# Three blocks of a selective scan: where GpSimd's additions and TensorE's convolution stand in the order of the state stage

## The chip, the cores and the metric

One core of a Trainium2 chip. The metric is the device time of one execution of the whole program in microseconds, median of the runs.

## What is computed

An image batch x of 16 x 28 x 28 x 32 passes through four layers, each added to x and each fed by a group norm of it: window attention, a gated convolution with a selective state space, a triangle product, and a gated recurrence. The change is in the second layer alone. Cut to what matters, for a sequence of L = 784 positions, D = 32 channels, N = 8 states:

```python
x1 = silu(conv3x3_depthwise(grouped_1x1(x, w1)))
u, z = in_proj(x1)
u = silu(causal_conv1d(u, 3 taps) + conv1d_b)
dt, Bm, Cm = split(u @ x_proj_w.T)
delta = softplus(dt @ dt_proj_w.T + dt_proj_b)
# for each position, in order:
h = exp(delta * A) * h + (delta * u) * Bm        # D x N
y = sum_n(h * Cm)
# behind the scan:
y = (y + u * D_param) * silu(z)
x1 = layernorm(out_proj(y)) * gamma + beta
out = grouped_1x1(x1 * silu(grouped_1x1(x, w2)), wout)
```

## The kernel before

Partitions are 4 groups of 32 channels, each group with images of its own, so the 16 images are four blocks of T = 784 columns. In the state stage, about 135 to 285 us of the span, the blocks c = 0..3 follow each other, and each has eight slots n = 0..7, one for each state. Slot (c, n) is:

- TensorE, `spread(c, n, h)`, L1339: row n of B spread over the channels, a matmul for each half h of the columns. It reads BCf, the rows of B and C of a block, in three bfloat16 pieces, and waits for `g_low`, the last step of `split(c)`. Half 0 also waits for the first scan half of the slot before, half 1 for its second (both blocks share one place in PSUM).
- VectorE, `times_b` (L1965) and `scan` (L1977), for each half: DU times the spread row in place, then the scan with the decay dA as factor. The first half also needs the decay from ScalarE (`decays`, L826) and that product n of four slots ago has been taken.
- DMA: `c_rows` on the SP queue (L428) copies row n of C out of BCf to all 32 channels of each group, 392 KB, into one of four buffers Cs. It waits for the product of four slots ago. Between these issues stand the twelve copies SX<-XP (L418) that each later block's 3x3 convolution reads.
- GpSimd, `times_c(c, n)`, L534: hC = Hs x Cs. It needs the row (`s_cs`), the scan (`v_s`) and the total of three slots ago (`y_s`). In this document it is product (c,n).
- TensorE, `total(c, n)`, L1343: hC added up over n in PSUM. When total(c,7) is done, VectorE's `outputs(c)` reads the sum (L1994, then L1997).

Everything that the next block needs is made beside these slots: on TensorE conv (L1278, 24 matmuls a half, from 12 in the program), inner (L1290), gate, delta, x_b (L1263, L1303), each put by hand between spreads and totals; on ScalarE their activations, each group behind a load of its table. Softplus of block k is made of max(v, 0), log(u) with u = 1 + exp(-|v|), and the rounding rest of u: `remainder(k)` on VectorE (L1942) gives `rest`; GpSimd adds the logarithm (`plus_log`, L539) and then subtracts the rest (`delta`, L544, which releases `v_dl`). `v_dl` is what the decays of block k and VectorE's `delta_u(k)` (L2006: DU = DL x US) wait for. GpSimd's `split(k)` (L518, L520) makes the three pieces of B. `scaled` (L551) and VectorE's `norm` (L1988), which waits for it, belong to the layer norm of the block two back, `residual` to its output.

Each engine runs its own list in the written order, and each waits by semaphores alone, so where a step stands in a list decides what is held up behind it. GpSimd's list between product (i,4) and product (i,7) was:

```python
# i = 0: 4, 5, plus_log(1), delta(1), split(1), 6, 7
# i = 1, 2: 4, split(i+1), plus_log(i+1), delta(i+1), 5, 6, scaled(i-1), 7
```

VectorE has delta_u(1) behind slot (0,7) in block 0, and delta_u(i+1) between slots (i,6) and (i,7) in blocks 1 and 2.

Of the kernel before, what the change touches and what calls it, by code (L numbers as in the profile page):

```python
# [8 lines left out]
ALU = mybir.AluOpType  # L9
# [31 lines left out]
def build(nc, a, out):  # L41
    ctx = ExitStack()
    with ctx:
# [423 lines left out]
        def _(eng):  # L467
# [46 lines left out]
            def split(k):  # L514

                eng.wait_ge(c_["xB"], k + 1)
                two, one = BCf[0:2 * C, k % 2, :], BCf[0:C, k % 2, :]
                eng.tensor_tensor(two, two, upper(two), ALU.subtract).then_inc(g_mid, 1)  # L518
                eng.wait_ge(g_mid, k + 1)
                eng.tensor_tensor(one, one, upper(one), ALU.subtract).then_inc(g_low, 1)  # L520
# [15 lines left out]
            def plus_log(k):  # L536
                eng.wait_ge(a_m, k + 1)
                eng.wait_ge(a_l, k + 1)
                eng.tensor_tensor(DL[:, k % 2, :], DL[:, k % 2, :], sp[:, SP_L, :], ALU.add).then_inc(g_ml, 1)  # L539

            def delta(k):
                eng.wait_ge(v_cc, k + 1)
                eng.wait_ge(g_ml, k + 1)
                eng.tensor_tensor(DL[:, k % 2, :], DL[:, k % 2, :], rest, ALU.subtract).then_inc(v_dl, 1)  # L544
# [41 lines left out]
            def pool_ssm(i):  # L586
                if i < J - 1:
                    times_c(i, 0, 1, 2, 3, 4)
                    if i == 0:
                        times_c(0, 5)  # L590
                        plus_log(1)
                        delta(1)
                        split(1)
                    else:
                        split(i + 1)
                        plus_log(i + 1)
                        delta(i + 1)
                        times_c(i, 5)
                    times_c(i, 6)
# [43 lines left out]
        def _(eng):  # L643
# [237 lines left out]
            def act_ssm(i):  # L881
                if i == 0:
# [14 lines left out]
                    decays(1, 0, 1)  # L897
# [4 lines left out]
                    decays(1, 2, 3)  # L902
# [181 lines left out]
        def _(eng):  # L1084
# [293 lines left out]
            def pe_ssm(i):  # L1378

                if i == 0:  # L1380
# [29 lines left out]
                    total(0, 4)  # L1410
                    spread(1, 0, 0)
                    conv(2, 1)
                    spread(1, 0, 1)
                    total(0, 5)
                elif i == 1:
                    spread(1, 1, 0)
                    inner(2, 0)
                    spread(1, 1, 1)
                    inner(2, 1)
                    spread(1, 2, 0)  # L1420
                    total(0, 6)
                    spread(1, 2, 1)
                    total(0, 7)
                    gate(1)
                    spread(1, 3, 0)
                    delta(2, 0)
                    delta(2, 1)
                    spread(1, 3, 1)
# [839 lines left out]
```

## Time and profile before

| | us |
|---|---|
| Median of 3 runs (all: 428.93, 429.76, 434.81) | 429.76 |
| The profiled execution | 428.19 |
| Its span, first to last instruction | 426.2 |
| TensorE busy in the span | 370.1 |
| VectorE busy | 315.3 |
| ScalarE busy | 286.0 |
| GpSimd busy | 163.2 |

The profile has the span, and 2.0 us of the execution's time lie around it. Engines in its rows: PE is TensorE, PEld its weight loads, DVE VectorE, ACT ScalarE, POOL GpSimd, SP the queue that issues DMAs. L534 is line 534 of the program.

### The profile page before, as it was taken

To read this page: it belongs to the slowest core of one execution; us is meant where nothing else is said; L and a number is where in the kernel's file an instruction comes from. 1 tells how busy PE (TensorE), PEld (TensorE's weight loads), DVE (VectorE), ACT (ScalarE), POOL (GpSimd) and SP (SyncE) were. 2 spreads that over 40 slices of the span, in tenths; PEclk is the share of its full clock that TensorE was granted. 3 is DMA by queue.
4 is the path that set the end of the run, shared out by engine and by line. 5 is a ranking of instruction groups with operands and counts; after the bars stand their busy time and mean duration, and the time that the engine had idled before them with its cause. 6 is when DMAs were issued, how large, how long until landed. Compare 5 with 4: busy or idle time off the path is not lost.

```text
span 426.2 us, 11110 instructions
## 1 busy us (share of the span) xinstructions
PE 370.1 (87%) x4065; PEld 252.5 (59%) x4065; DVE 315.3 (74%) x637; ACT 286.0 (67%) x600; POOL 163.2 (38%) x138
## 2 busy tenths in 40 slices
PE   5889999999998797698898776898978989999996
PEld 5667777777764342254354342443954569888885
DVE  2889886788746899589799899895658957555554
ACT  3599899999858684559859773359974354444443
POOL 7314313323103256755974988961622400000000
PEclk9999999999999999699999996999999989999999
DMA  7120000004133354263222222200020001111111
GB/s 160 9 21 7 2 0 1 0 0 100 32 70 89 118 137 123 109 163 114 102 101 104 102 98 102 75 0 0 11 67 2 2 1 23 16 22 22 22 22 27
DMA packets 28671, 23.17 MB, mean 54 GB/s; under 512 B 21105, under 2 KB 22897, under 8 KB 28641
## 3 DMA queue, kind: packets, MB, share of 16 engines
q1 hardware_dynamic: 28244, 22.73, 19.5%
q8 instruction: 18, 0.29, 0.3%
q10 hardware_dynamic: 396, 0.05, 0.1%
q14 instruction: 13, 0.10, 0.1%
HBM read 2.00 MB, written 1.61 MB: 8 GB/s over the span
## 4 chain that ended last, share of the span: by engine, by line
PE 35%; DVE 28%; issue 17%; ACT 9%; POOL 7%; DMA 3%; DVEq 1%; SPq 1%; ACTq 0%; POOLq 0%
PE pair L1670 7%; DVE pair L1965 5%; DVE Ts L1856 3%; PE pair L1658 3%; PE pair L1126 3%; PE pair L1177 3%; DVE stats L1744 3%; PE pair L1166 2%; DVE Hs L1977 2%; PE pair L1290 2%; PE pair L1185 2%; PE pair L1278 2%; DMA vec<-in_L_conv_b_qkv 2%; PE pair L1148 2%; POOL hC L534 2%
## 5 line engine op out<-in xcount | busy, mean ns | idle before, releaser
L534 POOL TENSOR_TENSOR hC<-Hs,Cs 128x784 f32<-128x784 f32 x31 | 63.5, 2051 | 44.2 <-DVE Hs L1977 27.3
L502 POOL TENSOR_TENSOR Km<-Ks,mask 128x784 f32<-128x784 f32 x16 | 24.1, 1506 | 68.7 <-ACT Ks L709 68.7
L1343 PE MATMUL pair<-hC,ident 128*128 128x392 f32 x128 | 49.2, 509 | 0.0
L1850 DVE TENSOR_REDUCE mx<-pair 128x8 f32<-128x392 f32 x64 | 32.9, 555 | 16.3 <-PE pair L1126 16.2
L1965 DVE TENSOR_TENSOR pair<-DU,pair 128x392 f32<-128x392 f32 x64 | 35.5, 555 | 8.9 <-PE pair L1339 8.8
L1339 PE MATMUL pair<-BCf,sel 96*128 96x392 bf16 x64 | 21.9, 348 | 22.5 <-DVE Hs L1977 17.9
L1166 PE MATMUL pair<-ident,Pr 128*128 128x128 f32 x256 | 37.5, 279 | 2.4 <-issue 1.2
L1670 PE MATMUL pair<-hst,BD 128*128 128x112 f32 x224 | 37.6, 299 | 2.2 <-DVE Rt L2237 0.4
L1166 PEld LDWEIGHTS pair<-ident,Pr 128*128 128x128 f32 x256 | 28.2, 141 | 13.2 <-issue 12.2
L1977 DVE TENSOR_TENSOR_SCAN Hs<-dA,Hs,pair 128x392 f32<-128x392 f32 x32 | 32.9, 1030 | 3.6
L1670 PEld LDWEIGHTS pair<-hst,BD 128*128 128x128 f32 x224 | 30.0, 195 | 9.3 <-DVE hst L2231 5.5
L826 ACT ACTIVATE dA<-DL,Aneg 128x784 f32<-128x784 f32 x32 | 29.1, 941 | 7.9 <-POOL DL L544 6.3
L1977 DVE TENSOR_TENSOR_SCAN Hs<-dA,pair 128x392 f32<-128x392 f32 x32 | 31.1, 970 | 4.2
L1339 PEld LDWEIGHTS pair<-BCf,sel 96*128 96x128 bf16 x64 | 6.2, 98 | 46.9 <-issue 39.2
L696 ACT ACTIVATE Pr<-Ts 128x392 f32<-128x392 f32 x64 | 31.5, 547 | 3.2 <-DVE Ts L1856 2.5
L1658 PE MATMUL pair<-XN,BD 128*128 (+1 forms) x224 | 31.8, 286 | 1.8 <-ACT XN L1047 1.8
L1343 PEld LDWEIGHTS pair<-hC,ident 128*128 128x128 f32 x128 | 24.7, 197 | 14.4 <-issue 4.2
L1856 DVE TENSOR_TENSOR Ts<-pair,mx 128x392 f32<-128x392 f32 x64 | 32.8, 553 | 0.0
L687 ACT ACTIVATE PT<-pair 128x392 f32<-128x392 f32 x64 | 29.6, 496 | 4.1 <-PE pair L1166 3.0
L1658 PEld LDWEIGHTS pair<-XN,BD 128*128 128x128 f32 x224 | 28.0, 196 | 2.3 <-ACT XN L1047 2.3
L1067 ACT ACTIVATE gates<-pair 128x112 f32<-128x112 f32 x28 | 7.4, 263 | 29.0 <-PE pair L1670 29.0
L2218 DVE SCALAR_TENSOR_TENSOR prods<-gates 128x112 f32<-128x112 f32 x28 | 7.7, 275 | 24.1 <-ACT gates L1067 24.1
(254 smaller groups left out, 842.1 us busy)
## 6 DMA issues: line engine op xcount, KB each, us to landing
Cs<-BCf SPq DMA_DIRECT2D x32, 392.0 KB
SX<-XP SPq DMA_DIRECT2D x48, 112.2 KB
XT<-in_x SPq DMA_DIRECT2D x4, 392.0 KB, 6.8
out<-Os SPq DMA_DIRECT2D x28, 56.0 KB, 1.7
AD<-Aa SPq DMA_DIRECT2D x4, 196.0 KB
NB<-in_L_conv_x_proj_w SPq DMA_DIRECT2D x4, 3.0 KB
DW<-in_L_conv_dw SPq DMA_DIRECT2D x4, 1.1 KB
W<-in_L_conv_w_qkv ACTq DMA_DIRECT2D x1, 48.0 KB
```

What stands on the lines that cost most here:

```text
L534: eng.tensor_tensor(hC[:, i % NHC, :], Hs[:, i % NHS, :], Cs[i % NCS][:, :], ALU.mult).then_inc(v_c, 1)
L687: eng.activation(PT[:, g].rearrange("p a b (o q) -> p (a b o) q", o=2), banks[5 + (par + 1 + g) % 2][:, :].rearrange("p (m k) -> p m k", k ...
L696: eng.activation(Pr[:, par, g, :, 0:WT], Ts[:, g, :, :], ACT.Exp).then_inc(exp_r, 1)
L826: eng.activation(dA[:, n % NA, :], DL[:, c % 2, :], ACT.Exp, scale=Aneg[:, n:n + 1]).then_inc(a_da, 1)
L1166: ins = eng.transpose(bk[:, P * k:P * k + P], pg, ident[:, :])
L1343: return eng.matmul(STATES[:, h, :], ident[:, :], src[:, columns(h)], start=first, stop=last)
L1658: eng.matmul(zb[k].rearrange("p (b n) -> p b n", b=J), BD[:, U_X + k, :], xt, start=False, stop=False, skip_group_check=True)
L1670: eng.matmul(zb[k], BD[:, U_M + k, :], hst[:, 1 - par, :], start=False, stop=True, skip_group_check=True).then_inc(done, 1)
L1850: eng.tensor_reduce(mx[:, g, :], banks[g][:, 0:392].rearrange("p (m k) -> p m k", k=WT), AX.X, ALU.max).then_inc(max_r, 1)
L1856: eng.tensor_tensor(Ts[:, g, :, :], banks[g][:, 0:392].rearrange("p (m k) -> p m k", k=WT), bcast(mx[:, g, :], 2, WT), ALU.subtract).then_ ...
L1965: eng.tensor_tensor(SPREAD[:, columns(h)], DU[:, c % 2, columns(h)], SPREAD[:, columns(h)], ALU.mult).then_inc(v_b, 1)
L1977: eng.tensor_tensor_scan(Hs[:, i % NHS, columns(h)], dA[:, n % NA, columns(h)], SPREAD[:, columns(h)], h0, ALU.mult, ALU.add).then_inc(v_s, 1)
```

## The change

GpSimd's order: at every boundary the two softplus additions come right behind product (i,4), then the split, then products 5, 6 and 7. In block 0 product (0,5) stood ahead of them; in blocks 1 and 2 the split did. The two additions change places: the rest is subtracted first, which needs `remainder`, and the logarithm is added last, which needs ScalarE's logarithm; the last still releases `v_dl`. The sum is the same up to rounding.

ScalarE: the decay (1,2) stands ahead of the silu group instead of behind it.

TensorE: between the spreads of slots (1,0), (1,1) and (1,2) the convolution of block 2 no longer stands as a whole half. conv(2,1) is put in three single taps (8 of the 24 matmuls each), inner(2,0) and inner(2,1) in two taps and one tap, and totals (0,5) to (0,7), gate(1) and delta(2) move by one place.

```diff
--- before.py
+++ after.py
@@ -533,15 +533,15 @@
                         eng.wait_ge(y_s, i - NHC + 1)
                     eng.tensor_tensor(hC[:, i % NHC, :], Hs[:, i % NHS, :], Cs[i % NCS][:, :], ALU.mult).then_inc(v_c, 1)
 
-            def plus_log(k):
+            def minus_rest(k):
                 eng.wait_ge(a_m, k + 1)
+                eng.wait_ge(v_cc, k + 1)
+                eng.tensor_tensor(DL[:, k % 2, :], DL[:, k % 2, :], rest, ALU.subtract).then_inc(g_ml, 1)
+
+            def delta(k):
                 eng.wait_ge(a_l, k + 1)
-                eng.tensor_tensor(DL[:, k % 2, :], DL[:, k % 2, :], sp[:, SP_L, :], ALU.add).then_inc(g_ml, 1)
-
-            def delta(k):
-                eng.wait_ge(v_cc, k + 1)
                 eng.wait_ge(g_ml, k + 1)
-                eng.tensor_tensor(DL[:, k % 2, :], DL[:, k % 2, :], rest, ALU.subtract).then_inc(v_dl, 1)
+                eng.tensor_tensor(DL[:, k % 2, :], DL[:, k % 2, :], sp[:, SP_L, :], ALU.add).then_inc(v_dl, 1)
 
             def scaled(m):
 
@@ -586,17 +586,10 @@
             def pool_ssm(i):
                 if i < J - 1:
                     times_c(i, 0, 1, 2, 3, 4)
-                    if i == 0:
-                        times_c(0, 5)
-                        plus_log(1)
-                        delta(1)
-                        split(1)
-                    else:
-                        split(i + 1)
-                        plus_log(i + 1)
-                        delta(i + 1)
-                        times_c(i, 5)
-                    times_c(i, 6)
+                    minus_rest(i + 1)
+                    delta(i + 1)
+                    split(i + 1)
+                    times_c(i, 5, 6)
                     if i:
                         scaled(i - 1)
                     times_c(i, 7)
@@ -894,12 +887,12 @@
                     copy_bc(1)
                     exponents()
                     decays(0, 7)
-                    decays(1, 0, 1)
+                    decays(1, 0, 1, 2)
                     silu_x2(1)
                     silu_conv(2, 0)
                     silu_conv(2, 1)
                     exponents()
-                    decays(1, 2, 3)
+                    decays(1, 3)
                 elif i < J - 1:
                     if i == 2:
                         silu_x2(2)
@@ -1408,24 +1401,28 @@
                     conv(2, 0)
                     spread(0, 7, 1)
                     total(0, 4)
+                    conv(2, 1, (0,))
                     spread(1, 0, 0)
-                    conv(2, 1)
+                    conv(2, 1, (1,))
                     spread(1, 0, 1)
+                    conv(2, 1, (2,))
                     total(0, 5)
                 elif i == 1:
                     spread(1, 1, 0)
-                    inner(2, 0)
+                    inner(2, 0, (0, 1))
                     spread(1, 1, 1)
-                    inner(2, 1)
+                    inner(2, 0, (2,))
+                    total(0, 6)
                     spread(1, 2, 0)
-                    total(0, 6)
+                    inner(2, 1, (0, 1))
                     spread(1, 2, 1)
+                    inner(2, 1, (2,))
                     total(0, 7)
+                    spread(1, 3, 0)
                     gate(1)
-                    spread(1, 3, 0)
                     delta(2, 0)
+                    spread(1, 3, 1)
                     delta(2, 1)
-                    spread(1, 3, 1)
                     total(1, 0)
                     spread(1, 4, 0)
                     x_b(2)
```

## Rows read from the trace of the kernel before

**Rows 1.** The page's part 4, the chain that ended last: shares by engine.

```profile
PE 35%; DVE 28%; issue 17%; ACT 9%; POOL 7%; DMA 3%; DVEq 1%; SPq 1%; ACTq 0%; POOLq 0%
```

**Rows 2.** Stretches: us, busy of PE, PEld, DVE, ACT, POOL, PEclk, DMA, GB/s.

```profile
166.00:180.00 14.00, 9.31 (x57) 3.27 (x58) 8.45 (x11) 4.81 (x7) 12.14 (x7) 0.79 0.26 101
180.00:196.00 16.00, 15.14 (x48) 8.04 (x47) 13.83 (x17) 11.06 (x14) 5.83 (x4) 0.97 0.60 156
196.00:245.00 49.00, 41.80 (x168) 20.45 (x166) 42.88 (x52) 38.48 (x44) 37.69 (x21) 1.00 0.26 102
```

**Rows 3.** Wait table, 140 to 290 us: waiter, releaser, us, times, longest.

```profile
POOL hC L534 <- DMA Cs<-BCf: 5.7, 3, 3.0
...
DVE DU L2006 <- POOL DL L544: 3.0, 2, 2.2
```

**Rows 4.** Timeline of GpSimd, first boundary: start, us, instruction, [idle before <-releaser].

```profile
160.17 2.33 POOL L534 TENSOR_TENSOR hC<-Hs,Cs 128x784 f32<-128x784 f32 x1 [1.43 <-DMA Cs<-BCf]
165.47 1.84 POOL L534 TENSOR_TENSOR hC<-Hs,Cs 128x784 f32<-128x784 f32 x1 [2.98 <-DMA Cs<-BCf]
...
171.08 1.49 POOL L518 TENSOR_TENSOR BCf<-BCf 64x784 f32<-64x784 f32 x1
172.65 2.10 POOL L520 TENSOR_TENSOR BCf<-BCf 32x784 f32<-32x784 f32 x1
```

**Rows 5.** Timeline of TensorE, first boundary.

```profile
166.95 2.18 PE L1278 MATMUL pair<-SX,W 96*32 96x392 f32 x24 [0.33 <-DMA SX<-XP]
...
169.25 1.48 PE L1343 MATMUL pair<-hC,ident 128*128 128x392 f32 x4
174.80 0.51 PE L1339 MATMUL pair<-BCf,sel 96*128 96x392 bf16 x1 [4.07 <-POOL BCf L520]
175.24 4.15 PE L1278 MATMUL pair<-SX,W 96*32 96x392 f32 x24
```

**Rows 6.** Timeline of VectorE, first boundary.

```profile
171.17 2.23 DVE L2006 TENSOR_TENSOR DU<-DL,US 128x784 f32<-128x784 f32 x1
175.42 0.57 DVE L1965 TENSOR_TENSOR pair<-DU,pair 128x392 f32<-128x392 f32 x1 [2.02 <-PE pair L1339]
...
179.94 0.57 DVE L1965 TENSOR_TENSOR pair<-DU,pair 128x392 f32<-128x392 f32 x1 [2.84 <-PE pair L1339]
...
192.36 0.56 DVE L1965 TENSOR_TENSOR pair<-DU,pair 128x392 f32<-128x392 f32 x1
```

**Rows 7.** Timeline of GpSimd, second and third boundary.

```profile
198.95 2.43 POOL L534 TENSOR_TENSOR hC<-Hs,Cs 128x784 f32<-128x784 f32 x1 [1.29 <-DMA Cs<-BCf]
...
206.34 1.85 POOL L544 TENSOR_TENSOR DL<-DL,sp 128x784 f32<-128x784 f32 x1
208.17 4.38 POOL L534 TENSOR_TENSOR hC<-Hs,Cs 128x784 f32<-128x784 f32 x2
...
214.36 1.85 POOL L534 TENSOR_TENSOR hC<-Hs,Cs 128x784 f32<-128x784 f32 x1
...
233.85 2.43 POOL L534 TENSOR_TENSOR hC<-Hs,Cs 128x784 f32<-128x784 f32 x1 [1.32 <-DVE Hs L1977]
```

**Rows 8.** Timeline of VectorE, second and third boundary.

```profile
197.78 1.03 DVE L1977 TENSOR_TENSOR_SCAN Hs<-dA,Hs,pair 128x392 f32<-128x392 f32 x1
...
208.23 2.62 DVE L2006 TENSOR_TENSOR DU<-DL,US 128x784 f32<-128x784 f32 x1 [2.18 <-POOL DL L544]
...
217.14 1.01 DVE L1988 SCALAR_TENSOR_TENSOR nt<-nt,vec,X 128x784 f32<-128x784 f32 x1
...
243.12 2.63 DVE L2006 TENSOR_TENSOR DU<-DL,US 128x784 f32<-128x784 f32 x1 [0.79 <-POOL DL L544]
...
252.05 1.01 DVE L1988 SCALAR_TENSOR_TENSOR nt<-nt,vec,X 128x784 f32<-128x784 f32 x1
```

**Rows 9.** Timeline of TensorE, end of total(1,4) and an idle time of 3.35 us.

```profile
209.17 1.58 PE L1343 MATMUL pair<-hC,ident 128*128 128x392 f32 x4
...
247.49 0.33 PE L1339 MATMUL pair<-BCf,sel 96*128 96x392 bf16 x1 [3.35 <-DVE Hs L1977]
```

## The prediction

> **What bounds the kernel now.** I read the chain that ended last first, to see which engine to distrust: TensorE has 35% of it, VectorE 28% and issue gaps 17% [rows 1], so no single engine sets the time, and it has to be read stage by stage. The change touches the state stage alone, about 135 to 285 us of the span. There the table by stretches says three things [rows 2]: VectorE is busy 42.9 of 49 us between 196 and 245, GpSimd 37.7, and the DMA share stands at 0.26 with 101 or 102 GB/s in two of the three stretches, the third having the SX copies too. A flat rate is what a queue that never runs empty looks like. The only transfer there is the copy of a row of C into Cs, 392 KB, so one takes 401,408 bytes / 101 GB/s = 3.97 us, and a block of eight 31.8 us. The wait table then says who waits for what the change moves: VectorE 3.0 us in two waits for delta, GpSimd 5.7 us in three for Cs [rows 3].
>
> The timeline around each boundary between blocks shows where the end is set. **First boundary**: GpSimd stands idle 2.98 us before product (0,5) for its Cs row, and only then come both steps of delta and the split, which ends at 174.75 [rows 4]. TensorE, idle for 4.07 us, starts spread(1,0,0) at 174.80, and the conv behind it takes 4.15 us where the same 24 matmuls took 2.18 [rows 5]: the granted clock over 166 to 180 is 0.79 [rows 2]. VectorE waits 2.02 us and then 2.84 us for these spreads [rows 6]. **Second**: GpSimd goes without idling from product (1,4), 198.95, to the end of product (1,7), 216.21 [rows 7]. VectorE waits 2.18 us for delta and then needs 2.62 us for delta_u [rows 8]. **Third**: the same, with a wait of 0.79 us [rows 8]. From delta_u to delta_u it is 34.9 us, against the 31.8 us that the eight rows of Cs need.
>
> One mechanism has to be priced with them. delta_u takes 2.23 to 2.63 us, and it ends about 0.85 us after the GpSimd instruction that was running when it started: split's first part ends at 172.57, delta_u at 173.40; product (1,5), at 1.85 us, ends near 210.0, delta_u at 210.85. The GpSimd instruction behind is stretched in turn (split's second part 2.10 us, its first 1.49) [rows 4, 6 to 8]. So the two engines take turns, instruction by instruction, and one that waits gets in at the next end. The Trainium skill (SBUF — State Buffer, "SBUF: two separate sides") calls this an exclusive lock on a port pair held for the whole instruction by a GpSimd operation or a VectorE one with two SBUF inputs; the trace agrees: of delta_u's 2.62 us only the last 0.85 lie outside the product.
>
> **First boundary, after.** Products (0,0) to (0,4) end at 162.5 (160.17 + 2.33) [rows 4]; now the subtraction of rest (its input, remainder(1), stands ahead of slot (0,5) on VectorE and is there), the addition of the logarithm and the split follow at once, in the time that was spent waiting for Cs. Their prices are 1.85 us for each addition and 1.49 for each part of the split [rows 4, 7], together with small gaps 6.9 us: delta is there at 166.4 to 166.9 and the split at 169.5 to 170.0, instead of 174.75. Products 5, 6 and 7 follow, to 176.3, with the turn of delta_u between. Nothing waits for them that early: total(0,5) runs behind the conv. On TensorE total(0,4) ends near 170.7, one tap of conv is a third of 2.18, 0.73 us [rows 5], so spread(1,0,0) runs near 171.5, and nothing lets the clock fall. VectorE finishes delta_u near 172.7 (it waits behind a product instead of the split) and starts the first slot then, not at 175.42: 2.7 us. The wait of 2.84 us inside that slot [rows 6] goes, since one tap, not a whole slow half, stands between the two spreads. In the next two slots the same work of inner, four of six matmuls ahead of the second spread and two behind, leaves TensorE as the bound for about 0.6 us, and total(0,7) ends near 183.6. outputs(0) follows, and slot(1,3) starts near 186.5 against 192.36 [rows 6]. Sum: 5.9 us. Decay (1,2), moved ahead of the table switch, costs the end nothing: silu_conv(2,0) behind it is not needed before inner(2,0), near 175.5.
>
> **Second boundary, after.** Here I follow the Cs rows. The copies run in order on a queue that is never empty from 166 to 245 [rows 2], so issuing one earlier does not land it earlier. The anchors are the two products that started when their row had landed: (0,5) at 165.47 and (1,4) at 198.95 [rows 4, 7]. Seven rows at 3.97 make 27.8 of these 33.5 us, the twelve SX copies of the third conv the other 5.7. None of this work is removed. So product (1,4) starts near 199.0 again, although VectorE now reaches it 5.9 us sooner. From there GpSimd is the bound, without a gap: product 200.9, rest 202.7, logarithm 204.7 (delta; before 208.2), split's first part 206.2, the turn of VectorE for delta_u 207.0, split's second part 208.5, products 5 and 6 at 212.2, scaled(0) 214.1. norm(0) on VectorE needs scaled(0), and product (1,7) needs nothing, so it starts first and norm gets its turn at 215.9. Before, norm ran 217.14 to 218.15 [rows 8]. Of the 5.9 us 1.3 are left. That is the step on which the forecast rests.
>
> From there the rows land at 198.9 + 3.97 for each further one: (2,2) at 222.7, (2,4) at 230.7. Product (2,2) would be ready about 223; if its row is a little later, VectorE's second step of outputs(1) gets in ahead and saves 0.9 more. So the gain is 1.3 to 2.2.
>
> **Third boundary, after.** Product (2,4), at 233.85 [rows 7], moves by the same 1.3 to 2.2, within what its row allows. The additions now come ahead of the split, so delta is there near 238.5 and VectorE, which arrives at 241.0 or a little sooner, has no wait (0.79 saved). It has to let split's second part end, near 241.6, and is done at 242.5, where it was done at 245.75 [rows 8]: 3.2. Then norm(1) again meets a running product, (2,7), to about 250.0, and ends near 250.9 against 253.06 [rows 8]: 2.0 to 2.7 left. The last block is not edited and starts that much earlier; its stages behind are one chain and move with it. Sum: **2.4 us**. The profiled execution took 428.19 us (span 426.2), so 425.8; the median of the runs shown is 429.76, 1.6 above it, and I take the sum from the median: **427.4 us**.
>
> **Bounds.** For what the trace does not show: who gets the turn at norm. If VectorE, each norm is 1.85 us earlier, at most 3.7 in all; if the turn at delta_u goes to split's second part as well, each of the two later boundaries is 1.6 us dearer, 3.2 in all. With both ends the gain is 6.1 down to -0.8. The middle is nearest to the rows: a product started at 208.17, right at the end of the addition that released delta_u, and delta_u at 208.23 came too late and had to wait for it, then got in ahead of the next product [rows 7, 8]. norm stands to scaled as that delta_u to its addition.
>
> The Trainium skill (DMA: Bandwidth & Descriptors, "Rules for kernel authors") says that a copy whose outermost dimension is shorter than 16 is confined to that many of the 16 DMA engines. The Cs copy starts from four partitions, and the share of 0.26 agrees. By that page's 27 GiB/s for an engine, a row would be an estimated 3.5 us instead of 3.97, and row (1,4) could land some 3 us sooner; the row of the trace decides. That case is the first rival.
>
> **Rivals.** *The copies do not hold.* If row (1,4) lands as early as VectorE wants it, near 193.2, the 5.9 us stay and each later boundary adds its wait (2.18 and 0.79), less the turns lost at norm (1.8 and 1.0, half of the first given back by a shorter delta_u): 5.9 + 0.8 + 0.7 = 7.4, 422.4 us. For it: the scan that product (1,4) also needs ended at 198.81 [rows 8], so the row may have landed well before, and the DMA be named wrongly. Against it: the flat rate.
> *GpSimd takes it all back.* Product (1,7) ended at 216.21, and its list of work from 199 on is unchanged in length; only the 0.6 us of product (1,4)'s own turn (2.43 against 1.85) is removed. If norm(0) and norm(1) wait behind it and nothing is gained at outputs(1) or at the third delta_u, 0 to 1 us is left: 429.2 us.
> *Slower: TensorE's clock falls at the later boundaries.* With the split behind delta, spread(2,0,0) can start only at 208.5, while TensorE's last work ahead of it, total(1,4), ended at 210.75 before [rows 9] and ends up to 5.9 us earlier now, near 204.9: 3.6 us idle. At 174.80, after 4.07 us, its spread ran at the clock's lower level of 1.2 GHz (0.51 us); after 3.35 us, at 247.49, it was at the full 2.4 GHz (0.33) [rows 5, 9]. So 3.6 us can go either way. A fall costs what it cost at the first boundary, the wait of 2.84 us [rows 6], and the late split 1.6: 4.4 us for each boundary. One gives 431.8, both 436.2.
> *The change does not do what it says*: the split is held by something else than product (0,5), 429.8; the split's end and the spread's start, 0.05 us apart [rows 4, 5], leave it little.
>
> **Chances.** The forecast 0.50 (426.0 to 428.8); the copies do not hold 0.20; GpSimd takes it back 0.18; slower 0.08; nothing 0.04. About 2%, 8.6 us, is what a measurement of this kernel can tell from no change. Faster than that needs the first rival and both turns at norm, 0.07; slower needs both falls of the clock and more such waits behind them, 0.02. The range takes in the first rival and stops short of the falls: 422.0 to 430.3.
>
> **What would show it.** Right: in the changed kernel TensorE's stretch 166 to 180 has a clock near 1.0, spread(1,0,0) starts near 171.5, slot(1,3) near 186.5; product (1,4) still starts within 1 us of 199.0, again after a wait for Cs; norm(0) takes more than 1.5 us. Wrong: product (1,4) before 196; a clock below 0.9 between 203 and 212; slot(1,3) later than 189, which would mean that the taps between the spreads cost what the earlier split gives.

## The result and the profile after

| | before | after |
|---|---|---|
| Median, us | 429.86 of 4 runs (428.93 to 434.81) | 438.9 of 4 runs (436.74, 438.36, 439.44, 440.16) |
| The profiled execution and its span | 428.19, 426.2 | 440.16, 438.1 |
| Ratio over all executions (of the medians alone 1.021) | | 1.018, 95% interval 1.009 to 1.027 |

The forecast was 427.4 us, at most 430.3. A second set of twelve executions of the changed kernel (after_again, below) has a median of 436.9 us beside 429.44 of the kernel before: ten lie from 436.1 to 440.1 us, two at 427.2 and 430.2. By their medians the change costs 7.5 to 9 us. Counted as slow, being over 1.5% above the fastest of their set, the ten would fall out and leave two that are no different from the kernel before (0.999, 0.993 to 1.004), but all four of the first set lie where the ten do and none of 85 executions of the kernel before is above 434.81, so they are taken as the kernel's own time.

**The chain that ended last, shares by engine**, and two of its lines, of the kernel after. It answers to [rows 1]: TensorE has 42% instead of 35, the DMAs 5 instead of 3, the queue that issues them 4 instead of 1.

```profile
PE 42%; DVE 28%; issue 12%; ACT 6%; DMA 5%; SPq 4%; POOL 1%; DVEq 1%; ACTq 0%; POOLq 0%
```
```profile
191.66 11.78 DMA SX<-XP
...
209.41 7.60 DVE DU L2003
```

**Stretches** of the kernel after, the three of [rows 2] and the next one: us, busy of PE, PEld, DVE, ACT, POOL, clock, DMA share, GB/s.

```profile
166.00:180.00 14.00, 13.60 (x72) 5.35 (x73) 12.60 (x17) 9.72 (x12) 10.86 (x7) 0.88 0.35 111
180.00:196.00 16.00, 14.80 (x49) 8.18 (x48) 14.55 (x19) 10.50 (x14) 6.11 (x3) 1.00 0.51 134
196.00:245.00 49.00, 36.19 (x137) 17.38 (x136) 37.93 (x40) 29.70 (x35) 28.21 (x16) 0.86 0.26 100
245.00:269.00 24.00, 16.59 (x50) 8.56 (x50) 22.24 (x21) 14.23 (x17) 16.99 (x12) 0.86 0.20 75
```

Up to 196 it goes the way that was forecast: VectorE is busier and the clock higher than before, 0.88 instead of 0.79 in the first stretch (near 1.0 was forecast; it is 1.00 in after_again). From 196 on every engine does less in the same 49 us (GpSimd 28.2 instead of 37.7) and the clock falls to 0.86. After 245 even the Cs queue is no longer full, 75 GB/s: something holds up VectorE, and the products that take the copies with it.

**First boundary.** Timelines of GpSimd, TensorE and VectorE, answering to [rows 4 to 6]:

```profile
162.25 2.43 POOL L534 TENSOR_TENSOR hC<-Hs,Cs 128x784 f32<-128x784 f32 x1 [1.31 <-DVE Hs L1974]
...
170.13 1.48 POOL L520 TENSOR_TENSOR BCf<-BCf 32x784 f32<-32x784 f32 x1
```
```profile
174.11 0.35 PE L1332 MATMUL pair<-BCf,sel 96*128 96x392 bf16 x1
```
```profile
173.79 2.28 DVE L2003 TENSOR_TENSOR DU<-DL,US 128x784 f32<-128x784 f32 x1
...
187.57 0.56 DVE L1962 TENSOR_TENSOR pair<-DU,pair 128x392 f32<-128x392 f32 x1
```

This execution is already 2.08 us late at product (0,4), 162.25 against 160.17, ahead of the first edited step. TensorE's lower clock in 140 to 146 (0.50; 1.00 before) doesn't explain it: in after_again, without that fall, the product started at 162.13, and in the eight kernels of the experiments between 159.39 and 162.79. The profile of the kernel before is one of the earlier ones. Even so the split ends at 171.61, not 174.75, no wait is left inside slot (1,0), and slot (1,3) starts at 187.57, not 192.36: 4.8 us gained, 6.9 with the late start taken off. The forecast was 5.9, but its parts came otherwise: slot (1,0) starts at 176.11, against 175.42 before [rows 6], which with the late start is 1.4 of the 2.7 us expected there, and the other 5.5 are gained behind it. Of these, 0.9 were in no sum: the second step of outputs(0) takes 0.97 us instead of 1.88, since no product runs when it asks.

**Second boundary.** GpSimd, VectorE and TensorE, answering to [rows 7 to 9]:

```profile
202.07 1.83 POOL L534 TENSOR_TENSOR hC<-Hs,Cs 128x784 f32<-128x784 f32 x1 [3.26 <-DMA Cs<-BCf]
...
205.87 1.86 POOL L544 TENSOR_TENSOR DL<-DL,sp 128x784 f32<-128x784 f32 x1
207.69 1.49 POOL L518 TENSOR_TENSOR BCf<-BCf 64x784 f32<-64x784 f32 x1
209.26 1.49 POOL L520 TENSOR_TENSOR BCf<-BCf 32x784 f32<-32x784 f32 x1
210.71 3.67 POOL L534 TENSOR_TENSOR hC<-Hs,Cs 128x784 f32<-128x784 f32 x2
214.35 1.83 POOL L551 TENSOR_TENSOR nt<-cS,rs 128x784 f32<-128x784 f32 x1
220.33 1.84 POOL L534 TENSOR_TENSOR hC<-Hs,Cs 128x784 f32<-128x784 f32 x1 [4.15 <-issue]
```
```profile
191.90 0.97 DVE L1974 TENSOR_TENSOR_SCAN Hs<-dA,pair 128x392 f32<-128x392 f32 x1 [0.59 <-ACT dA L819]
...
199.66 0.97 DVE L1974 TENSOR_TENSOR_SCAN Hs<-dA,pair 128x392 f32<-128x392 f32 x1 [0.42 <-ACT dA L819]
207.78 0.57 DVE L1962 TENSOR_TENSOR pair<-DU,pair 128x392 f32<-128x392 f32 x1 [7.15 <-PE pair L1332]
208.46 1.03 DVE L1974 TENSOR_TENSOR_SCAN Hs<-dA,Hs,pair 128x392 f32<-128x392 f32 x1
209.41 7.60 DVE L2003 TENSOR_TENSOR DU<-DL,US 128x784 f32<-128x784 f32 x1
...
250.05 7.10 DVE L2003 TENSOR_TENSOR DU<-DL,US 128x784 f32<-128x784 f32 x1
```
```profile
203.47 3.92 PE L1271 MATMUL pair<-SX,W 96*32 96x392 f32 x24 [5.83 <-DMA SX<-XP]
...
218.74 0.49 PE L1332 MATMUL pair<-BCf,sel 96*128 96x392 bf16 x1 [4.45 <-DVE Hs L1974]
...
258.88 0.48 PE L1332 MATMUL pair<-BCf,sel 96*128 96x392 bf16 x1 [6.95 <-DVE Hs L1974]
```

Two things are new. First, conv(3,0), which stands ahead of spread(1,6,1) on TensorE, waits 5.83 us for the copies SX<-XP, runs at the lower clock, and VectorE waits 7.15 us for the spread behind it. Second, delta_u takes 7.60 and 7.10 us instead of 2.62 and 2.63 [rows 8]. An operation of 0.95 us that is shown with 7.60 is one that waits inside: delta_u(2) asks at 209.41, during the second step of the split, and ends at 217.01, 0.83 us after scaled(0). Two products and scaled have passed it. It is let in when GpSimd has to stop, since product (1,7) needs a scan that stands behind delta_u. delta_u(3) asks at 250.05, again in the second step of a split (249.43 to 250.91). TensorE, with no spread to make, stands idle 4.45 and 6.95 us and comes back at its lower clock.

The sum from slot (1,3) to the end of delta_u(2) was 192.36 to 210.85, 18.49 us, and is 187.57 to 217.01, 29.44: 10.95 more. The wait for the spread is 7.15, delta_u 4.98, the waits for ScalarE's decays 0.59 and 0.42, and the wait for delta, 2.18, is gone: 10.96. From there to the end of delta_u(3) it is 40.14 us instead of 34.90. Together: -4.8 + 10.95 + 5.24 = 11.4 of the 11.9 us between the two spans.

### The profile page after: what moved, and what is told of

Same layout as the page of the kernel before. It is cut to its first block, busy times and chain, and to the rows that moved or that the text cites. A ratio compares the mean times of both kernels' runs of the same rounds, so it can differ in the third digit from the quotient of the medians.

```text
span 438.1 us, 11110 instructions
## 1 busy us (share of the span) xinstructions
PE 380.0 (87%) x4065; PEld 256.5 (59%) x4065; DVE 324.1 (74%) x637; ACT 286.7 (65%) x600; POOL 159.8 (36%) x138
## 4 chain that ended last, share of the span: by engine, by line
PE 42%; DVE 28%; issue 12%; ACT 6%; DMA 5%; SPq 4%; POOL 1%; DVEq 1%; ACTq 0%; POOLq 0%
PE pair L1667 6%; PE pair L1271 4%; DVE pair L1962 4%; DVE DU L2003 3%; SPq L418 3%; PE pair L1159 3%; PE pair L1655 3%; DMA SX<-XP 3%; PE pair L1283 3%; DVE Ts L1853 3%; DVE Hs L1974 3%; PE pair L1170 2%; PE pair L1119 2%; DVE stats L1741 2%; PE pair L1336 2%
## 5 line engine op out<-in xcount | busy, mean ns | idle before, releaser
L534 POOL TENSOR_TENSOR hC<-Hs,Cs 128x784 f32<-128x784 f32 x31 | 60.5, 1955 | 59.4 <-DVE Hs L1974 21.9
L1336 PE MATMUL pair<-hC,ident 128*128 128x392 f32 x128 | 51.2, 526 | 0.0
L1332 PE MATMUL pair<-BCf,sel 96*128 96x392 bf16 x64 | 23.0, 365 | 20.5 <-DVE Hs L1974 20.3
L1159 PE MATMUL pair<-ident,Pr 128*128 128x128 f32 x256 | 38.6, 285 | 2.1 <-issue 1.2
L1667 PE MATMUL pair<-hst,BD 128*128 128x112 f32 x224 | 37.7, 299 | 2.1 <-DVE Rt L2234 0.4
L1159 PEld LDWEIGHTS pair<-ident,Pr 128*128 128x128 f32 x256 | 29.3, 144 | 12.7 <-issue 11.5
L1271 PE MATMUL pair<-SX,W 96*32 96x392 f32 x192 | 22.1, 600 | 7.7 <-DMA SX<-XP 5.8
```

Source lines behind the costliest of these rows:

```text
L534: eng.tensor_tensor(hC[:, i % NHC, :], Hs[:, i % NHS, :], Cs[i % NCS][:, :], ALU.mult).then_inc(v_c, 1)
L1159: ins = eng.transpose(bk[:, P * k:P * k + P], pg, ident[:, :])
L1271: ins = eng.matmul(row_groups(pairs[place("conv", b)][:, :, 0:HT], h)[g], W3[:, y, :], rows[:, g, 14 * h + y:14 * h + y + 14, 0:W], start= ...
L1336: return eng.matmul(STATES[:, h, :], ident[:, :], src[:, columns(h)], start=first, stop=last)
L1667: eng.matmul(zb[k], BD[:, U_M + k, :], hst[:, 1 - par, :], start=False, stop=True, skip_group_check=True).then_inc(done, 1)
```

## The experiments

Their question: what makes the loss, the wait for SX, the turns at delta_u, or the place of the split? Each ratio, with its 95% interval in brackets, is to the kernel before, run beside it (medians 429.96, 429.44 and 429.78 in the three sets).

### One part undone: e1_split_first

```diff
-                    minus_rest(i + 1)
-                    delta(i + 1)
-                    split(i + 1)
+                    if i: split(i + 1)
+                    minus_rest(i + 1)
+                    delta(i + 1)
+                    if i == 0: split(1)
```

> The changed kernel, with the split of blocks 2 and 3 again ahead of the two additions on GpSimd; everything at the first boundary and on TensorE and ScalarE stays changed. Theory A (VectorE's delta_u starves because it asks for its turn while a part of the split, on 32 or 64 partitions, runs and full products follow without a gap): delta_u of the second and third boundary falls from 7.60 and 7.10 us to about 2.6, since it now meets a full product, as before the change; the wait for the SX copies (5.83 us) stays; 432 to 435 us. Theory B (GpSimd simply always goes first while it has work): delta_u stays at 5 us or more and the time at 438. Rival C (only the falls of TensorE's clock cost the time): delta_u's length changes nothing in the time, 437 to 440.

430.0 us (427.6 to 431.1, 10 runs), ratio 1.000 (0.997 to 1.003): the loss is gone, and the time is 2 us below the range expected. delta_u takes 2.63 us at both later boundaries; the wait for SX is 1.44 us. Here full-width additions and products stand around the request, not the split. VectorE's first delta_u is the exception; its request fell into the first of three products that followed a split without a pause, and it was let in behind the third:

```profile
172.43 4.71 DVE L2006 TENSOR_TENSOR DU<-DL,US 128x784 f32<-128x784 f32 x1
```

### The SX copies ahead of the Cs rows: e2_sx_early

```diff
-            shifted_copies(3, (0,))
-            c_rows(1, 3)
-            shifted_copies(3, (1,))
-            c_rows(1, 4)
-            shifted_copies(3, (2,))
-            c_rows(1, 5, 6, 7)
+            shifted_copies(3)
+            c_rows(1, 3, 4, 5, 6, 7)
```

> The changed kernel, with all twelve SX copies for the convolution of block 3 issued in a run ahead of the Cs rows (1,3) and (1,4) instead of between them. Theory A': the copies land in the order of one busy queue, so those behind row (1,4) cannot land before it; issued earlier they are there before conv(3,0), its wait of 5.83 us goes and VectorE's wait of 7.15 us for the spread behind it falls below 1; the time falls by 3 to 6 us, 433 to 436, with delta_u still at 5 us or more. Rival (the wait was no more than the Cs backlog, and product (1,4) and delta of block 2 are as late as before): conv(3,0) starts earlier and VectorE waits for delta instead, the time stays within 1.5 us of the changed kernel.

434.1 us (431.2 to 436.3, 10 runs), ratio 1.009 (1.005 to 1.012). The wait for SX is gone, but only about half of the loss, 4.2 us being left of it:

```profile
197.47 1.88 POOL L530 TENSOR_TENSOR hC<-Hs,Cs 128x784 f32<-128x784 f32 x1 [8.38 <-DMA Cs<-BCf]
201.45 1.85 POOL L530 TENSOR_TENSOR hC<-Hs,Cs 128x784 f32<-128x784 f32 x1 [2.10 <-DMA Cs<-BCf]
```
```profile
207.14 2.25 DVE L1999 TENSOR_TENSOR DU<-DL,US 128x784 f32<-128x784 f32 x1 [7.62 <-POOL DL L540]
216.28 4.34 DVE L1981 SCALAR_TENSOR_TENSOR nt<-nt,vec,X 128x784 f32<-128x784 f32 x1
244.70 7.14 DVE L1999 TENSOR_TENSOR DU<-DL,US 128x784 f32<-128x784 f32 x1
```

The wait only moved: what VectorE no longer waits for at the spread, it waits for at delta (7.62), as product (1,4) and delta behind it come when the queue has done its bytes. delta_u(2) then asks in the split's first step and takes 2.25 us, norm(0) behind it 4.34. The third boundary, far from any SX copy, still has a delta_u of 7.14 us. So the half that is left goes with the one long turn that is left; whether the other half is the turn or the wait, this run alone doesn't tell (e7 below does).

### GpSimd waits for VectorE: e3_yield, e6_yield_conv_late

```diff
                     split(i + 1)
+                    if i:
+                        eng.wait_ge(v_du, i + 2)
                     times_c(i, 5, 6)
```

> The changed kernel, with GpSimd waiting for delta_u of blocks 2 and 3 before it goes on from the split to product 5, so that VectorE cannot be passed over. Theory A or B: delta_u takes at most 2.4 us (the rest of a split part and 0.9), products 5 to 7 come a little later and nothing on VectorE waits for them; 430 to 433 us. Rival C (clock, or the products' lateness, is what costs): 437 us or more.

427.4 us (424.5 to 430.4, 10 runs), ratio 0.992 (0.988 to 0.996), below the 430 to 433 expected. GpSimd stands still for 0.9 us and VectorE has its turn:

```profile
206.91 1.48 POOL L520 TENSOR_TENSOR BCf<-BCf 32x784 f32<-32x784 f32 x1
209.31 3.68 POOL L534 TENSOR_TENSOR hC<-Hs,Cs 128x784 f32<-128x784 f32 x2 [0.91 <-DVE DU L2005]
```
```profile
207.88 1.35 DVE L2005 TENSOR_TENSOR DU<-DL,US 128x784 f32<-128x784 f32 x1
...
242.84 1.69 DVE L2005 TENSOR_TENSOR DU<-DL,US 128x784 f32<-128x784 f32 x1
```

e6 adds to it that conv(3,0) stands behind spread(1,6,1) and total(1,3):

```diff
-                    conv(3, 0)
                     spread(1, 6, 1)
                     total(1, 3)
+                    conv(3, 0)
```

> The kernel with GpSimd waiting for delta_u ahead of product 5 in blocks 1 and 2 (e3), and conv(3,0) on TensorE behind spread(1,6,1) and total(1,3) instead of ahead of them. If the SX copies' landing costs the time only through the spread behind the conv, VectorE's wait of 4.22 us for that spread goes and the time falls by a further 2 to 4 us, to 423 to 426. Rival (VectorE then waits as long for delta of block 2, which hangs on product (1,4) and its Cs row near 199): within 1 us of e3, 427.4.

428.3 us (426.8 to 431.8, 12 runs), ratio 0.997 (0.994 to 1.000): the rival's outcome. VectorE's wait for the spread is gone and a wait of 3.53 us for delta stands in its place. With the turns given back, nothing is to be had from the place of conv(3,0).

### The split's place in the kernel before: e4_split_last_only

```diff
                     else:
-                        split(i + 1)
                         plus_log(i + 1)
                         delta(i + 1)
+                        split(i + 1)
                         times_c(i, 5)
```

> The kernel before, with one edit of the change alone: in blocks 1 and 2 GpSimd makes the split behind the two additions, not ahead of them (the additions in their old order, the first boundary and TensorE as before). Theory A (a chain that holds a part of the split lets VectorE in only where GpSimd pauses): delta is there 3 us sooner and delta_u meets a part of the split at both boundaries and takes 6 to 8 us instead of 2.62; with the 2.18 and 0.79 us waits gone the time rises by 3 to 8 us, to 433 to 438. Rival (it is the first boundary's gain that brings VectorE early, and the split's place alone is harmless): within 1.5 us of 430.

430.5 us (426.2 to 432.4, 10 runs), ratio 1.001 (0.997 to 1.004): the loss that I expected did not come. The split stands behind the two additions as in the changed kernel, and delta_u takes 1.98 and 0.95 us in the profile. It asks at 207.09 and 241.68 and is not in the second step of a split when it does. Only at the first boundary, where the order is that of the kernel before, does the request (174.54) fall into it, and there it takes 5.77 us:

```profile
174.34 1.48 POOL L520 TENSOR_TENSOR BCf<-BCf 32x784 f32<-32x784 f32 x1
175.79 3.68 POOL L534 TENSOR_TENSOR hC<-Hs,Cs 128x784 f32<-128x784 f32 x2
```
```profile
174.54 5.77 DVE L2006 TENSOR_TENSOR DU<-DL,US 128x784 f32<-128x784 f32 x1
```

So the order makes the loss possible, and the moment at which VectorE asks decides. The kernel before has the same weak spot at its first boundary; in its profile VectorE asked at 171.17, in the split's first step, and was let in between the two steps [rows 4, 6], where GpSimd waits for its own result. At this boundary the long turn costs nothing that shows in the time: delta_u took 4.71 us in e1, 5.77 here and 5.90 in e8, kernels of 428 to 430.5 us. It stands in the place of other waits: VectorE's 2.02 and 2.84 us for the spreads [rows 6] aren't there in e4, and in e1 product (1,4) still waits 4.02 us for its row.

### The changed kernel once more: after_again

> The changed kernel once more. Its first profile had TensorE at the lower clock already from 140 to 146 us, ahead of the first edited step, and every step some 2 us late from there. If that fall belongs to the kernel it stays; if not, a profile without it starts product (1,4) near 199.5 and ends near 436, still slower than before.

Twelve runs: ten from 436.1 to 440.1 us, and two at 427.2 and 430.2. The profile is of one of the ten (span 434.9). TensorE's lower clock in 140 to 146 is not in it (granted clock 1.00), but product (0,4) is as late (162.13), product (1,4) starts at 202.15 and not at the 199.5 expected, and both long turns are there, 7.14 us each:

```profile
209.99 7.14 DVE L2003 TENSOR_TENSOR DU<-DL,US 128x784 f32<-128x784 f32 x1
...
248.47 7.14 DVE L2003 TENSOR_TENSOR DU<-DL,US 128x784 f32<-128x784 f32 x1
```

The two short executions have no profile. That VectorE asked at another moment there would fit, but is not shown.

### The turn by itself: port, port2, port3

A kernel that computes nothing of the reference (its output is zeros). GpSimd runs a chain on 784 columns without a pause, and VectorE asks once for a product of two SBUF tiles, 0.97 us when alone. The letters: F is a full product, H and Q the split's steps on 64 and 32 partitions (fp32 minus a bfloat16 view, in place), U the same form on 128 partitions and M on 96, N is Q written to another tile, I and q are fp32 products on 32 partitions (I in place), S a product of half the columns, w a wait for GpSimd's own last result.

> A kernel that computes nothing of the reference and writes zeros: twenty chains of GpSimd operations without gaps (F on 128 partitions x 784, H on 64, Q on 32, w a wait for the one before), and for each one VectorE operation with two SBUF inputs that asks while the chain runs. Theory A: in FFFF VectorE gets in behind the operation that runs (under 2.8 us), in QFFFF and HFFF, asked while Q or H runs, it waits for the end of the chain (over 7 us); a w behind the short operation lets it in. Theory B (GpSimd always first): over 5 us in FFFF too. Theory D (first come, first served, whatever the width; the kernel's long delta_u has another reason): under 2.8 us in all.

> Again chains of GpSimd operations beside one VectorE operation, nothing of the reference. S is 128 partitions with half the columns, q 32 partitions in the form of F, U 128 partitions in the form of the split. Theory A (it is the width in partitions): qFFFF waits for the end of the chain (over 7 us), UFFFF and SFFFF let VectorE in after one operation (under 2.8), QFwFFF at the w, QFFFF asked in the second F still at the end; in FFFFFF VectorE gets in wherever it asks, and FFFQF, asked in the second F, too. Rival (it is the split's form with its bfloat16 operand): UFFFF waits too and qFFFF doesn't. Rival (it is a short operation at the head): SFFFF waits too.

> A kernel of its own that computes nothing of the reference (its output is zeros): chains of GpSimd operations on 784 columns without a pause, while VectorE asks for one operation with two SBUF inputs. F is a full multiplication, Q the split's step on 32 partitions in place (fp32 minus a bfloat16 view). QFFFF again 9.4 us. N is Q written to another tile, I is 32 partitions in place with fp32 inputs alone, M is the split's step on 96 partitions. If partitions and form together do it, N and M behave as Q (9.4) and I lets VectorE in (2.6); if writing in place does it, I and M give 9.4 and N 2.3 to 2.6. Of QHFFF, QUFFF (U is the form on 128 partitions), QSFFF (S is a half width multiplication) and QqFFF (q is a multiplication on 32 partitions): if a Q at the head spoils the turn until the next pause, all take until the end of the chain, 7.5 to 9.5. QFFFFFF (13 us) shows whether it is the whole chain or a fixed time; FQFFF asked in Q 7.0, UFFFF asked in the first F 1.5, NFFFF asked in the first F 7 or 1.5, by the same rules.

| Chain, VectorE asks in | its product took, us | let in |
|---|---|---|
| FFFF, first F | 2.27, 1.51 when asked later in it | behind that F |
| FwFFF, FFHwQFF, FFFFFF, first F | 2.59 | behind that F |
| FFFFFF, second, third, fourth F | 1.49, 1.50, 1.49 | behind that F |
| QFFFF and HFFFF, Q or H | 9.41, 9.41 | at the chain's end |
| QFFFFFF, Q | 12.99 | at the chain's end |
| QFFFF, first and second F | 7.12, 5.31 | at the chain's end |
| FQFFF, Q | 7.12 | at the chain's end |
| HwQFFF, H; Q | 2.24; 7.49 | behind H; chain's end |
| QFwFFF, first F | 1.74 | at the pause |
| NFFFF and MFFFF | 9.41, 9.41 | at the chain's end |
| IFFFF, qFFFF, UFFFF, SFFFF | 2.64, 2.64, 2.25, 1.76 | behind the first |
| QHFFF, QSFFF | 9.07, 8.58 | at the chain's end |
| QqFFF | 7.62 | ahead of the last F |
| QUFFF | 2.30 | behind Q |
| UFFFF, first F; NFFFF, first F | 1.75; 7.12 | behind that F; chain's end |
| qqqqqq, first q | 2.58 | behind that q |

Every chain was run twice in a kernel, with the same outcome to 0.05 us, save the first one of a kernel, in which VectorE started ahead of GpSimd and took 0.97 us (0.98 in port3); the table has the second run of these. In three more chains (FFHwQFFF, FSFFF, FFFQF) the request fell right onto the end of an F and took 0.97 us; they decide nothing. Two of the chains in the timelines of port and port3, QFFFF and the same with I in Q's place:

```profile
15.75 1.48 POOL L88 TENSOR_TENSOR gs<-gs 32x784 f32<-32x784 f32 x1
15.83 9.41 DVE L113 TENSOR_TENSOR vd<-va,vb 128x784 f32<-128x784 f32 x1 [0.19 <-POOL tick L76]
17.20 7.20 POOL L83 TENSOR_TENSOR gd<-ga,gb 128x784 f32<-128x784 f32 x4
```
```profile
26.99 1.82 POOL L97 TENSOR_TENSOR gs<-gs,ga 32x784 f32<-32x784 f32 x1
27.06 2.64 DVE L128 TENSOR_TENSOR vd<-va,vb 128x784 f32<-128x784 f32 x1 [0.19 <-POOL tick L76]
```

So my theory of the width alone fell (q, I), that of the form alone fell (U), and it is the two together: a step on fewer than 128 partitions that subtracts a bfloat16 view, followed without a pause, and VectorE is passed over. In place or not doesn't matter (N). What in the form does it, the subtraction, the bfloat16 type or the view of every second element, these chains don't separate, since they change together. Why a U behind it restores the turn and an F, H or S doesn't is open.

### A pause alone: e7_pause, and two more: e8_before_yield, e9_yield_norm

e7 is the changed kernel with GpSimd waiting for its own split, not for VectorE:

```diff
                     split(i + 1)
+                    eng.wait_ge(g_low, i + 2)
                     times_c(i, 5, 6)
```

> The changed kernel with one wait more: GpSimd waits for the end of its own split before product (i,5), at every boundary. It does not wait for VectorE. Theory (VectorE is passed over because products follow the split's narrow step without a pause): delta_u takes at most 2.7 us at each boundary instead of 7.1, no spread runs at the lower clock behind it, and the time is 427.5 to 430.5, although the wait for SX stays at 2 to 6 us. Rival (the wait for SX ahead of spread(1,6,1) makes the loss, the turns only follow): delta_u is short, but the time stays above 433. Second rival (a pause between instructions is not enough, GpSimd must stand still until delta_u has begun): delta_u still takes 4.5 us or more at one boundary, 431 to 438.

**426.8 us** (424.4 to 430.1, 12 runs), ratio 0.993 (0.990 to 0.996), so with that one wait 10 to 12 us below the changed kernel's two medians. The profile is of its slowest run, 430.14, and is all the more telling for it: the waits ahead of delta_u are longer than in the changed kernel.

```profile
204.54 1.83 POOL L534 TENSOR_TENSOR hC<-Hs,Cs 128x784 f32<-128x784 f32 x1 [4.12 <-DMA Cs<-BCf]
...
211.71 1.48 POOL L520 TENSOR_TENSOR BCf<-BCf 32x784 f32<-32x784 f32 x1
213.27 4.30 POOL L534 TENSOR_TENSOR hC<-Hs,Cs 128x784 f32<-128x784 f32 x2
```
```profile
210.88 0.57 DVE L1963 TENSOR_TENSOR pair<-DU,pair 128x392 f32<-128x392 f32 x1 [10.12 <-PE pair L1333]
...
212.50 1.52 DVE L2004 TENSOR_TENSOR DU<-DL,US 128x784 f32<-128x784 f32 x1
...
245.42 1.98 DVE L2004 TENSOR_TENSOR DU<-DL,US 128x784 f32<-128x784 f32 x1
```

VectorE waits 10.12 us for the spread behind conv(3,0), which waits 8.41 us for SX; product (1,4) comes 2.5 us later than in the changed kernel; and again delta_u asks during the split's second step (211.71 to 213.19). Now it ends 0.83 us behind it. The lower clock at conv(3,0) is there too, with a granted clock of 0.56 in 203 to 212 (0.78 in the changed kernel), and this run is still 6.8 and 10.0 us below the changed kernel's two profiled ones. From the start of product (1,4) to the end of delta_u(2) it is 14.94 us in the changed kernel and 9.48 here; from there to the end of delta_u(3) 40.14 and 33.38. The rival, that the wait for SX makes the loss, expected over 433 us.

e8 is the kernel before with the wait of e3 behind `delta(i + 1)` in blocks 1 and 2; e9 is e3 with `eng.wait_ge(v_nt, i)`, a wait for norm(i-1), ahead of product (i,7).

> The kernel before with one wait more in blocks 1 and 2: GpSimd waits for delta_u(i+1) before product (i,5). Nothing of the change is in it. If the time that delta_u spends behind product (i,5) is on the path, delta_u takes 1.0 us instead of 2.62 at both boundaries and the time is 2.5 to 3 us below the kernel before, 426.5 to 427.5, so that the changed kernel with such a wait (427.4) has nothing from the change itself. Rival (GpSimd is the bound behind delta_u, and norm waits for it): what VectorE gains at delta_u it waits for at norm, 429 to 430, and the gain of the changed kernel with the wait comes from the change.

> The changed kernel with both waits: GpSimd waits for delta_u(i+1) before product (i,5), and for norm(i-1) before product (i,7). Theory (a product in front of norm costs VectorE its length, or several): norm takes 1.0 us at both boundaries instead of 2.6 to 3.8, and the time is 1.5 to 3 us below the one with the first wait alone, 424.5 to 426. Rival: product (i,7) comes some 3 us later, total(i,7) and outputs(i) wait for it, and the time is 427 to 429.5.

e8: 428.1 us (424.0 to 432.2, 12 runs), ratio 0.995 (0.992 to 0.998). delta_u takes 0.98 and 0.97 us instead of 2.62 and 2.63, but norm(0) and norm(1) 1.97 and 3.87 instead of 1.01 and 1.01 [rows 8], so both theories have a part: half of the saving is given back. norm(1) was passed over as well. It asks during product (2,7) and ends 0.84 us behind product (3,0), the next one, though GpSimd ran only full-width fp32 steps since its last pause, none of a split:

```profile
250.00 3.73 POOL L534 TENSOR_TENSOR hC<-Hs,Cs 128x784 f32<-128x784 f32 x2
```
```profile
250.70 3.87 DVE L1989 SCALAR_TENSOR_TENSOR nt<-nt,vec,X 128x784 f32<-128x784 f32 x1
```

The same happens in e3 (3.84 us) and e7 (3.62 us). So the split's form is one way to lose the turn, not the only one; the second has no experiment here.

e9: 426.2 us (423.4 to 429.2, 10 runs), ratio 0.993 (0.989 to 0.996). Its norms take 1.01 and 1.03 us, and product (1,7) stands 1.90 us. It can't be told from e3 or e7. e3, e7 and e9 are 2.6 to 3.5 us below the kernel before; e8 has 1.7 of that without the change, and its interval overlaps theirs, so that what the change itself is worth once the turns are mended, about 1 to 2 us, isn't told apart from nothing.

## Why the prediction was wrong

**The step that failed** is the one that I put as "the two engines take turns, instruction by instruction, and one that waits gets in at the next end". It rested on three requests, in the split's first step, in an addition's wake and in a full product [rows 4, 6 to 8], and was read as a rule for all. The split's second step, with products right behind it, is a place of GpSimd's list at which it doesn't hold (norm(1) in e3, e7 and e8 met another), and the change puts delta and the split in such an order that VectorE comes to delta_u just there. I allowed for "the turn at delta_u goes to split's second part as well" and priced it at 1.6 us a boundary. It cost 4.98 and 4.47 us at delta_u against before, and TensorE's idle time and lower clock behind it. e7 shows it: the wait for the split alone, which leaves all else in its order, brings the time to 426.8.

With a pause behind the split, then, the kernel takes about what the sum gave, 426.8 to 427.4 for 427.4. That is in part luck: 1.7 us of it come in e8 without the change, by turns that are better than the sum assumed, and a second step was left out of the sum.

**The omitted consumer.** I used the twelve SX copies as bytes that fill the queue and did not ask who waits for them. conv(3,0) does, it stands ahead of a spread, and with 5.9 us gained in front of it it meets its copies (they land at 203.43; it started at 201.67 before, without that wait, so they are also later here). What it made was a wait of 7.15 us of VectorE, the largest of the terms found. Most of it is no loss: the last SX copies land within 1.4 us of row (1,4) (conv(3,0) starts at 203.47, product (1,4) at 202.07), and delta can't be ready until 3.9 us of additions behind that product have run (203.87 to 207.73), whatever VectorE does. Taken away in e2 and e6, it came back as a wait for delta of 7.62 and 3.53 us. It costs through the moment at which it sets VectorE down at delta_u: at 209.41, 1.7 us after delta was ready (207.73) and in the wrong step of the split.

**What was right.** The first boundary: split at 171.61 with a late start of 2.08, forecast 169.5 to 170.0, and a gain of 6.9 for 5.9, though not by the parts forecast. The queue that holds: product (1,4) started after a wait for Cs, at 202.07 here, at 198.89 in e1, 199.73 in e3, 201.45 in e2 and 204.54 in e7, forecast 199.0, never near 193.2; the first rival is out. The Trainium skill (DMA: Bandwidth & Descriptors, "Specifications") gives about 27 GiB/s, 29 GB/s, for a DMA engine; the trace doesn't bear that out for these rows: 101 to 103 GB/s at a share of 0.26 of 16 engines, from 203 to 245 us in the kernel before, is about 25 GB/s each. Of the spread of starts, some 6 us, I had allowed 1, having anchored it on one profile: in e4 and e8, whose first boundary is that of the kernel before, the product started at 201.13 and 201.16.

**The rival of the slower side** had the right effect and the wrong cause. TensorE's clock does fall at both later boundaries (0.49 us at 218.74 and 0.48 at 258.88 for a spread), priced at 4.4 us a boundary. I had it from the late split. In the trace the idle time ahead of them ends with a scan behind the long delta_u, so the long turn is its cause here, and conv(3,0) is slow (3.92 us) behind its wait for SX.

**Three signs that I named failed as signs.** norm(0) and norm(1) take 1.01 us each: not as forecast, but because product (1,7) now comes so late that VectorE doesn't meet it. And product (1,4) "within 1 us of 199.0" was 3 us off while its step was right. And a clock below 0.9 between 203 and 212 came, 0.78, but stands in e7's profile too, with 0.56, where the loss is gone.

**Two sums were off** and changed nothing: the first rival's terms as named give 5.9 + 1.3 - 0.2 = 7.0, not 7.4, and the bound of -0.8 is 430.6, just outside the range that I gave.

## What to carry to other kernels

Where VectorE and GpSimd share a path, an order of instructions has a turn of its own: look at what GpSimd is running, and what follows it without a wait, at the moment at which VectorE asks, and price a missed turn at GpSimd's whole run up to its next wait, not at one instruction; it costs that only where VectorE wouldn't have waited anyway. A cheap wait of GpSimd for its own result behind a narrow mixed-type step gave the turn back here (e7). And before time is gained in front of a FIFO of copies, list every consumer of every transfer in it, not only the one whose bytes fill it.

## What the runs showed of the hardware

- In chains of full-width products alone, a VectorE product of two SBUF tiles that asks during one is let in behind it (1.5 to 2.6 us). If it asks during a step on 32 to 96 partitions that subtracts a bfloat16 view, or up to two products behind it, it is passed over by up to six products, 12.99 us, until GpSimd pauses; QUFFF and QqFFF are the exceptions tried. norm, a step of another form with two SBUF tiles, was passed over by a full-width product without such a step in e3, e7 and e8 (3.84, 3.62 and 3.87 us). The Trainium skill (SBUF — State Buffer, "SBUF: two separate sides") says that whoever starts first has the port pair for the whole instruction. The runs agree for one instruction; who is next it doesn't say, and it isn't always the one that waits.
- The same program gave two times, 427 to 430 and 436 to 440 us. The moment at which VectorE asks decides a turn (e4); that it also decides between the two times is not shown.
- How long TensorE was idle doesn't alone tell its clock: in e9 a spread ran at the full 2.4 GHz after an idle time of 4.40 us (0.33 us), in e3 one at 1.2 GHz after 2.55 us (0.49 us).

```profile
258.57 0.33 PE L1335 MATMUL pair<-BCf,sel 96*128 96x392 bf16 x1 [4.40 <-DVE Hs L1977]
```
```profile
256.39 0.49 PE L1334 MATMUL pair<-BCf,sel 96*128 96x392 bf16 x1 [2.55 <-DVE Hs L1976]
```
